# A six-sublayer decoder on one core: the loop over passes written out as four batches, lane 1 half a pass behind lane 0

## The reference

```python
x = _layernorm(x + _L0_attn_ref(x, ...))             # hyena: projection, 3-tap conv, long conv, gate
x = _layernorm(x + _L0_xattn_ref(x, ctx, mask, ...)) # cross attention over 77 context rows
x = _layernorm(x + _L0_ffn_ref(x, ...))              # quantised feed-forward, 128 -> 512 -> 128
x = _layernorm(x + _L1_attn_ref(x, ...))             # selective scan, 256 channels, 16 states
x = _layernorm(x + _L1_xattn_ref(x, ctx, ...))       # cross attention, 16 heads, q and k normalised
x = _layernorm(x + _L1_ffn_ref(x, ...))              # product-key experts, 1024 experts, 8 heads, top 8
```

## Time and profile before

| what | value |
|---|---|
| median of 3 runs | 1172.66 us (1167.64 to 1173.07) |
| profiled execution | 1170.97 us |
| its span, first to last instruction | 1169.3 us |
| mean granted TensorE clock | 0.868 |
| busy: PE, DVE, ACT, POOL | 839.9 (72%), 816.1 (70%), 701.5 (60%), 292.4 (25%) us |

### The profile page before, as it was taken

One profiled execution on the slowest core, in us unless ns is written; L12 is line 12 of the kernel. 1 busy time (PEld: TensorE's weight loads), 2 busy tenths in 40 slices (PEclk: granted clock), 3 DMA queues, 4 the chain that ended last, 5 costly groups with the idle time before them and its releaser, 6 DMA issues. The chain is left out here.

```text
span 1169.3 us, 12317 instructions
## 1 busy us (share of the span) xinstructions
PE 839.9 (72%) x3574; PEld 508.2 (43%) x3576; DVE 816.1 (70%) x1651; ACT 701.5 (60%) x2226; POOL 292.4 (25%) x170
## 2 busy tenths in 40 slices
PE   2561377999967589889825138499997748998883
PEld 2450235556656334435414124355574643435432
DVE  2268736888445699999717875488755567999993
ACT  1513359993598295685712053999547828595691
POOL 0011105886165100000000200288635620000000
PEclk9765597999999799999957558699998979999997
DMA  8100011320000000000010000132100000000000
GB/s 224 37 0 1 0 41 46 98 92 18 1 1 1 1 0 1 1 0 1 0 52 1 0 1 5 57 97 91 46 1 1 1 1 1 1 0 1 1 1 18
DMA packets 26816, 27.41 MB, mean 23 GB/s; under 512 B 7172, under 2 KB 17146, under 8 KB 26746
## 3 DMA queue, kind: packets, MB, share of 16 engines
q1 hardware_dynamic: 24776, 24.63, 7.2%
q10 hardware_dynamic: 1970, 1.97, 0.6%
HBM read 25.28 MB, written 1.31 MB: 23 GB/s over the span
## 5 line engine op out<-in xcount | busy, mean ns | idle before, releaser
L1502 POOL TENSOR_TENSOR rs<-ve,minus_half 128x4 f32<-128x4 f32 (+1 forms) x56 | 89.3, 1595 | 671.7 <-DVE ve L1145 582.5
L894 PE MATMUL ps<-mem,ident 128*128 128x512 f32 x512 | 230.9, 600 | 31.1 <-DVE mem L1471 30.5
L1105 ACT ACTIVATE mem<-mem 128x32 f32<-128x32 f32 x1024 | 217.8, 310 | 0.0
L926 ACT ACTIVATE mem<-ps 128x512 f32<-128x512 f32 (+7 forms) x108 | 66.1, 612 | 204.0 <-PE ps L900 58.5
L1517 POOL TENSOR_TENSOR mem<-mem 128x1024 f32<-128x1024 f32 x64 | 150.9, 2359 | 116.2 <-DVE mem L1318 115.9
L1318 DVE TENSOR_TENSOR_SCAN mem<-mem,ps 128x1024 f32<-128x1024 f32 x64 | 146.0, 2285 | 45.2 <-PE ps L735 45.1
L1471 DVE SCALAR_TENSOR_TENSOR mem<-mem 128x1024 f32<-128x1024 f32 x128 | 159.3, 1278 | 14.9 <-ACT mem L1105 13.4
L894 PEld LDWEIGHTS ps<-mem,ident 128*128 128x128 f32 x512 | 94.0, 190 | 167.0 <-issue 92.3
L742 PE MATMUL ps<-mem,ident 128*128 128x512 f32 x256 | 121.6, 602 | 0.0
L1073 ACT ACTIVATE mem<-ps,mem,rs 128x77 f32<-128x77 f32 x256 | 101.9, 444 | 20.1 <-DVE mem L1374 20.1
L1463 DVE TENSOR_TENSOR mem<-mem 128x1024 f32<-128x1024 f32 x96 | 113.0, 1217 | 0.7 <-DVE mem L1445 0.5
(11 more groups left out here) (217 smaller groups left out, 1209.0 us busy)
## 6 DMA issues: line engine op xcount, KB each, us to landing
mem<-bc_rows SPq DMA_DIRECT2D x64, 256.0 KB, 3.1
x<-in_x_dram SPq DMA_DIRECT2D x4, 256.0 KB, 3.5
out_dram<-x SPq DMA_DIRECT2D x4, 256.0 KB, 2.3
mask<-in_mask_BxSxS_ik_dram SPq DMA_DIRECT2D x4, 154.0 KB, 3.4
mem<-n_L_ffn_expert_down_dram SPq DMA_DIRECT2D x1, 512.0 KB
mem<-in_L_xattn_Wo_dram SPq DMA_DIRECT2D x1, 512.0 KB
mem<-in_L_xattn_Wv_dram ACTq DMA_DIRECT2D x1, 512.0 KB
a_q<-in_L_xattn_Wq_dram SPq DMA_DIRECT2D x1, 512.0 KB, 4.8
```

Source lines behind the costliest of these rows:

```text
L894: mm = pe.matmul(ps[:, j, :], ident[:], WH[s][:, h % WB, j * 512:(j + 1) * 512], start=(h == 0), stop=(h == PH - 1), skip_group_check=True)
L1105: ins = nc.scalar.activation(SVA[s][:, n % 2, i * NK:(i + 1) * NK], sims[:, 1, h, :], ACT.Identity, bias=sims[:, 0, h, i:i + 1])
L1502: nc.gpsimd.tensor_tensor(RS[s][0:rows, i * n:(i + 1) * n], VE[s][0:rows, i * n:(i + 1) * n], minus_half[0:rows, 0:n], ALU.pow)\
```

## The change

The loop is gone. Each engine's list now holds all four batches, two per lane one after the other, in a single block; semaphores are never cleared between them, and waits count on from a base per batch (`TURNS` says how often each semaphore rises in one batch). Every stage number is mapped by a table `CLOCK` to a number between 0 and 550, plus 550 for the second batch of a lane. `LAG = 270.0` is added for lane 1, so lane 1's first stages stand where lane 0 is in the middle of `cross1`, and lane 0's second batch follows its first with nothing between. `x` is loaded to a tile of its own (`xin`), for the next batch at the time of `bitffn`. Transfers, too, stand in one order by that number. The sublayers' instructions are the same; one interleaving number in `cross1` goes from 0.2 to 0.9.

```diff
+    def batch(self, sems, turns, s, n):
+        for name, of in sems.items():
+            key = self.key(of[s])
+            self.base[key] = n * turns[name]
+            self.seen[key] = 0
...
-        self.eng.wait_ge(sem, self.seen[key])
+        self.eng.wait_ge(sem, self.base.get(key, 0) + self.seen[key])
+
+    def reach(self, sem, n):
+        self.eng.wait_ge(sem, self.base.get(self.key(sem), 0) + n)
...
-    LAG = 0
+    LAG = 270.0
...
+        XI = lanes(sb, "xin", [P, NB, P])
...
+        CLOCK = [
+            [(0, 0), (1, 2), (2, 9), (3, 14), (4, 19), (5, 25)],
...
+            [(0, 98), (1, 100.5), (2, 108), (2.2, 122), (2.4, 126), (3, 130), (4.2, 136), (20, 225), (21, 231),
+             (22, 239), (23, 247)],
+            [(0, 250), (1, 252), (6, 268), (10, 270), (42, 325), (46, 330), (60, 335), (61, 340)],
+            [(0, 344), (3, 352), (10, 357), (18, 397), (30, 402), (38, 442), (50, 447), (58, 487), (70, 492),
+             (78, 532), (90, 539), (94, 541), (95, 545)],
+        ]
+        PASS = 550
...
-        def sublayers(phases):
+        def clock(n, stage):
+            points = CLOCK[n]
+            for (k0, t0), (k1, t1) in zip(points, points[1:]):
+                if stage <= k1:
+                    return t0 + (stage - k0) * (t1 - t0) / (k1 - k0)
+            return points[-1][1] + stage - points[-1][0]
+
+        def sublayers(phases, w):
             def program(s):
-                for n, phase in enumerate(phases):
-                    for stage in phase(s):
-                        yield 100 * n + stage
+                for b in range(B // LANES):
+                    w.batch(sg, TURNS, s, b)
+                    for n, phase in enumerate(phases):
+                        for stage in phase(s, b):
+                            yield PASS * b + clock(n, stage)
             return program
...
+                        def loads(b):
+                            i = LANES * b + s
+                            if b >= 1:
+                                sp.wait_ge(sg["x_ready"][s], (b - 1) * TURNS["x_ready"] + 2)
+                            sp.dma_start(XI[s][:], x[i].rearrange("(k p) d -> p k d", p=P))\
+                                .then_inc(sg["x_loaded"][s], 16)
...
+                            if b + 1 < B // LANES:
+                                yield PASS * b + clock(2, 1)
+                                loads(b + 1)
...
-                            yield 14.5 + 4 * u + off + 0.2 * n
+                            yield 14.5 + 4 * u + off + 0.9 * n
...
-        with nc.Fori(0, B // LANES) as it:
-            body(it)
-            for q in lane_sems:
-                nc.gpsimd.sem_clear(q)
-            nc.all_engine_barrier()
+        body()
+        for q in lane_sems:
+            nc.gpsimd.sem_clear(q)
+        nc.all_engine_barrier()
```

More of the change, by code:

```diff
@@ L791, in memory, with scan_memory, cross1 @@
                         mm.then_inc(G("k_ready", s), 1)
-                def scan_memory(s):
-                    yield from merged(scan(s), memory(s))
-                def cross1(s):
+                def scan_memory(s, b):
+                    yield from merged(scan(s, b), memory(s, b))
+                def cross1(s, b):
                     ps = PS[s]
@@ L912, in experts @@
                             expert_inputs(k + 1)
-                in_turn(sublayers([hyena, cross0, bitffn, scan_memory, cross1, experts]))
+                in_turn(sublayers([hyena, cross0, bitffn, scan_memory, cross1, experts], w))
         def act_program(block):
@@ L1167, in bank, with hyena @@
                     return PS[s][:, n, :].rearrange("p (k d) -> p k d", k=NB)
[L1169 removed]
+                def hyena(s, b):
                     ps = PS[s]
                     yield 1
[L1172 removed]
+                    w.next(G("x_loaded", s), 16)
                     for j, c in enumerate((0, 2)):
@@ L1277, in bitffn, with scan @@
                     new_x(s)
-                def scan(s):
+                def scan(s, b):
                     ps = PS[s]
                     yield 1
-                    for j, b in enumerate([1, 2, 3, 0]):
+                    for j, at in enumerate([1, 2, 3, 0]):
                         w.next(G("u_ready", s))
@@ L1334, in scan, with memory @@
                     new_x(s)
-                def memory(s):
+                def memory(s, b):
                     ps = PS[s]
@@ L1539, in program @@
                         rsqrt(s, P, NB)
-                in_turn(program)
-        with nc.Fori(0, B // LANES) as it:
-            body(it)
-            for q in lane_sems:
-                nc.gpsimd.sem_clear(q)
-            nc.all_engine_barrier()
+                def program(s):
+                    for b in range(B // LANES):
+                        w.batch(sg, TURNS, s, b)
+                        for stage in stages(s):
+                            yield PASS * b + clock(int(stage // 100), stage % 100)
+                in_turn(program)
+        body()
+        for q in lane_sems:
+            nc.gpsimd.sem_clear(q)
+        nc.all_engine_barrier()
 _INS = ['x', 'ctx_1024', 'mask_BxSxS2_ik1', 'L0_attn_w_in', 'L0_attn_b_in', 'L0_attn_w_conv',
```

157 lines of the change are left out of this document (80 added, 77 removed), and 2 rows, old and new, of the table CLOCK.

## The result

| kernel | us, median | lowest to highest | ratio to before, 95% |
|---|---|---|---|
| before | 1171.66 | 1167.64 to 1173.07 | |
| changed | 1649.97 | 1646.18 to 1650.45 | 1.4083 (1.4041 to 1.4125) |

Slower, as forecast, but by 478 us where the forecast was 234: 1650 against 1405, and outside the range (1230 to 1475). The profiled execution has a span of 1648.3 us.

The account below looks back on a forecast made before the run. No engine was full; lanes waited on chains of short steps in the front sublayers, plus a seam. 39.3 + 362 + 234 + 213 + 359 + 183 + 13.7 = 1404.0 span; forecast 1405 us, range 1230 to 1475.

Parts of the forecast that it names:

- (iii): Middle stretch, one lane's scan beside the other's experts, three times: 133 + 93 + 133 = 359 us.
- Theory A: From the follow-up runs: the offset puts one lane's instructions behind the other's waits, and these chains are the loss.
- The seam: Gap between passes in which no engine but ACT works: goes whole, 17.8 us saved once.
- The lone lane, 362: Both ends, where one lane runs alone: chain of 75 + 25 + 62 + 14 + 68 + 118 = 362 us.
- everything is in one chain: ... with hops 8.2 us: Most scan steps beside experts: transposes, scan, thresholding, head sums and own sum follow one another, 8.2 us a step.
- (i): Middle stretch, cross1's half blocks beside the other lane's hyena and cross0: 78 us each, 234 for three.
- (ii): Middle stretch, start and first block of the experts beside bitffn's end and the scan's start: together 213 us.
- (iv): Middle stretch, last experts block beside the other lane's scan end, memory and cross1's start: together 183 us.
- followed in the same way: Sizing of (iv) by following pieces of the other lane's y, keys and values between 8 heads: 61 us against 51.
- Table loads: ACT's new list has 25 where 13 ran: 12 more by 1.28 us, 15.4 us busy.
- TensorE's clock falls too: Rival: a third of (iii) at 1.2 GHz, each step gains 1.5 us, 48 steps 73 us, 1478 in all; chance 0.12.
- the forecast's own loop of 133 us: Lane 1's scans beside lane 0's experts, first transposes to last: 133 us; in lockstep that work was worth 86.

Follow-up runs that it names:

- E1: The changed kernel with LAG = 0 instead of 270.0, both lanes again in lockstep: 1145.06 us, ratio 0.9773.
- E2: The changed kernel with TensorE's sums of an expert head (L943) standing 1.0 later in its list: 1500.04 us.
- E7: The changed kernel with LAG = 8.0 instead of 270.0, a small offset of lane 1: 1232.96 us.
- E8: The changed kernel with LAG = 30.0 instead of 270.0: 1343.08 us.
- E9: The changed kernel with LAG = 1100.0, so that no two batches overlap, one lane after the other: 1595.0 us.
- E5: The changed kernel with eight idle matmuls ahead of head sums from a block's second head on, none in lane 1's lone experts at the end: 1629.53 us.
- E6: E5 plus GpSimd's product on 32 of 512 columns in every step but the first two of each lane's first pass: 1592.51 us.
- E4: The changed kernel with GpSimd's product on 32 of 512 columns from the third step of each pass on: 1611.06 us.
- E12: E5 plus eight idle matmuls ahead of each half block's scores in cross1, in both lanes: 1627.92 us.

## Why the prediction was wrong

*Direction, structure.* Right: the lists make chains, (iii) above all, and the offset costs more than the seam gives. Theory A was shown by E1 (no offset, no loss) and E2 (one place in one list, 150 us); its narrow form, that the loss comes from a scan beside experts, was refuted by E7 and E8. (By its own steps the sum gives 1406 for the profiled execution and some 1407 for the median; 1405 was written, which changes nothing.)

*The seam.* "One seam's worth, 17.8." Measured 27 in E1. The step looked at time without work. VectorE was idle for 25.2 us, since the new pass also had transposes, projections and copies ahead of it; the traces show 21 to 24 of the 27.

*The lone lane, 362.* Measured 394.7, and 385 in the mean of E9. Front and scan start took 111.4 us for 75 + 25, with the clock at 0.56 (0.59 and 0.83 in these stages before); no run shows how much of it is the clock's. The scan loop was right (58.7 for 62). Cross1's start was 12 in the sum; from the last lone scan to the first maxima it took 38.4 us for 26: `x` is ready at 225.5, and TensorE turns it only at 234.4, behind the memory's keys and values. A lone half block took 5.7 to 6.8, in the mean 6.2, not 6.0, the long ones behind scores at the low clock. The experts took 126.0 for 118.

*(iii), 359.* Measured 442.0. The failed step is "everything is in one chain: ... with hops 8.2 us": its links were priced at the durations of lockstep. Two corrections to the durations carry most of it where lane 1 scans: the clock (E5, E6: 9.83 to 8.13 a step) and the shared port (E6, first against second pass: 14.41 to 9.39 in the worst step; some 2 us of that are the thresholding's, 3 the clock's, since H and Y behind the shorter wait ran at the higher level). With both gone the loop is 139.2 against 133. Where lane 0 scans, 116.2 was measured for 93, in steps of 6.6 to 12.2 where the forecast had none over 6.7. E6 still has 110.8 and six steps of 8.2 to 12.4, so there the chain itself was sized 18 short: the forecast names no step with a block's tail there, and the two that have one take 12.

*(i), (ii), (iv), 630.* Measured 758.7, 129 over, and neither E4, E5 nor E6 brings more than 18 of it back. (i) is 92.7 us in the mean. The same cross1 alone took 60.2, where the forecast had 56, so the other lane's pieces cost 32.5, where it had 22. The failed step is "followed in the same way": I added the pieces of the other lane that stand in a chain, but not what they wait for. One of (iv)'s places:

```profile
631.82 0.69 ACT L975 ACTIVATE mem<-ps 128x616 f32<-128x616 f32 x1 [2.28 <-PE ps L837]
634.65 6.87 ACT L1154 ACTIVATE mem<-mem 128x32 f32<-128x32 f32 x32
641.61 1.28 DVE L1522 SCALAR_TENSOR_TENSOR mem<-mem 128x1024 f32<-128x1024 f32 x1 [12.96 <-ACT mem L1154]
```

ScalarE's sums of the eighth head stand in its list behind the other lane's copies, these behind TensorE's L837, and these between two heads of the first lane. VectorE waits 12.96 us; in lockstep its waits for these sums added up to 13.4 in the whole kernel, here to 53.0. E2 takes 62 us from (ii) and (iv), which were 85 over, by the order alone: 31 of 51 and 31 of 34. So in (ii) the excess is mostly the order's. In (iv) E4 takes 17 of the same 34, so there order and port overlap. In (i) no run moved the length. The place shown in E12 has the same form: the other lane's scores and softmax were priced at their own 3.7 us, and with the wait for them the half block is 7.6 longer than alone, some 2 of it by the clock.

*Table loads.* 25 were forecast and 32 ran. Seven more at 1.28 us are 9 us of ScalarE's time; how much of it is on the path no run shows. As in rows 6, no drain shows: the load at 506.09 began 0.02 us behind the ACTIVATE ahead of it, and the next began 1.29 us later.

*The rivals.* "TensorE's clock falls too" was real: +1.5 us a step was forecast, +1.7 measured. I set it beside the main forecast as an alternative with 0.12, but it holds together with it. Even so 1478 was 172 short. The serial time was not among my cases, and I took lockstep's durations as if they held in a slower surrounding.

The fastest kernel of all is E1, at 0.977 of the time before.

## What to carry to other kernels

Where each engine works through one list, an offset between lanes is no free overlap: each instruction also waits for all that stands ahead of it. Before pricing an overlap, price the two pieces one after the other, and distrust a plan whose chain is longer than that sum: the forecast's own loop of 133 us was longer than its lone loop and two lone blocks, 62 + 2 x 25.5 = 113. And a duration taken from a full, fast stretch does not hold in a chain of waits: price the matrix work at both clock levels, and look which engine will run beside which.

## What the runs showed of the hardware

- *TensorE's clock.* At the two levels (1.2 and 2.4 GHz) the same four sums took 1.98 us (behind a wait of 1.40 or 1.83) and 3.78 us (behind one of 6.78), four scores 1.30 and 2.42. The wait just ahead does not decide alone. Behind 3.56 us the group at 456.89 took 1.98, while that at 474.90 took 3.00: it began at the higher level (granted 1.00 up to 475.7), fell to the lower (0.50 from 475.8), and the level was back at 1.00 from 479.2. Behind 2.98 us, at 514.44, a group took 3.78, and in E6, at 1196.76, one behind 3.09 took 1.98. Idle bf16 matmuls in the wait kept the higher level, but eight of them begun at the lower took 3.62 us instead of 1.89.
- *VectorE and GpSimd.* An operation with two SBUF inputs took 3.25 us instead of 1.20 to 1.28 when it began beside the product, the product 3.24 to 3.31 instead of 2.36 when it began beside such an operation. A scan, with one of its inputs in PSUM, was at 2.29 us always. The Trainium skill (SBUF — State Buffer, SBUF: two separate sides) says that these two engines share a pair of ports under an exclusive lock, which the first holds for its whole instruction, against a VectorE operation with two SBUF inputs. The trace agrees: the product begun at 441.38, 0.16 us behind the sum, ran 0.9 longer, about what the sum had left, and the thresholding begun at 442.45 ended 1.08 us behind the product's end (444.62).
- *A small GpSimd operation.* It shows the same from the other side. The product of 64 elements a partition (E4) took 0.32 or 0.33 us in the 19 cases without such a VectorE operation beside it, and 1.21 to 1.28 in the 37 cases where it began beside one (L1514 or L1522); all 37 ended 0.18 us behind that operation's end, as here, at 509.08 behind 508.89. So E4 shortened the product and did not take the meeting away; it left little for VectorE to wait for.

```profile
507.69 1.20 DVE L1514 TENSOR_TENSOR mem<-mem 128x1024 f32<-128x1024 f32 x1
507.86 1.22 POOL L1569 TENSOR_TENSOR mem<-mem 128x64 f32<-128x64 f32 x1 [3.42 <-DVE mem L1369]
```
